# Layer 0 in blocks of 512 tokens, three of them beside the first steps of a recurrence

## The reference, cut to what matters

```python
# x: (2, 1024, 256), N = 64 states
conv = conv_b + sum(x_pad[:, k:k+L, :] * conv_w[k, 0] for k in range(2))
proj = conv @ Wp + bp
B_t, C_t = softplus(proj[..., :N]), tanh(proj[..., N:])
u = x @ Ws + bs
decay = 1.0 + dt * A            # A = -softplus(A_log), dt = softplus(dt_log)
state = decay * state + dt * b_t * u_t      # step by step over 1024 tokens
y = c_t * state
x = x + real(ifft(fft(y @ Wo + bo) @ w)) + bias
```

```python
gate = sigmoid(h @ Wh.T + z_t @ Wz.T + b)
h = tanh(h * leak + gate * z_t)
```

## Time and profile before

| | us |
|---|---|
| median of 3 runs | 3188.67 |
| lowest and highest | 3188.18, 3189.39 |
| the profiled execution, its own time | 3185.09 |
| its span | 3183.8 |
| first `arg` (step 0) in it | 111.73 |
| first `arg` of step 60 in it | 199.50 |

### The profile page before, as it was taken

The page is one execution under the profiler, slowest core; times in us unless marked ns, Lnnn a source line. Parts: engine busy times, 40 slices in busy tenths (PEclk is TensorE's granted clock), DMA queues, the critical chain, the costliest instruction groups (busy, mean ns, idle before and its releaser), DMA issues.

```text
span 3183.8 us, 141437 instructions
## 1 busy us (share of the span) xinstructions
PE 2736.1 (86%) x55104; PEld 2214.4 (70%) x55104; DVE 2172.5 (68%) x13088; ACT 1572.4 (49%) x8437; POOL 338.1 (11%) x457
## 2 busy tenths in 40 slices
PE   4548989989899899998998989988649999979984
PEld 2337878888788888888888888887636666644331
DVE  2558888877777777777777666665437666666238
ACT  2244555556666666666665555543215555531115
POOL 0000010010100101101001010010113444420000
PEclk8555555555555555555555555555559999989997
DMA  2114223322222222322223000000357767332000
GB/s 80 44 53 129 71 84 92 87 64 68 89 89 82 91 63 91 99 80 89 69 88 108 7 17 7 14 17 3 119 189 226 229 193 213 92 129 106 0 0 27
DMA packets 170043, 270.36 MB, mean 85 GB/s; under 512 B 23289, under 2 KB 125580, under 8 KB 167076
## 3 DMA queue, kind: packets, MB, share of 16 engines
q1 hardware_dynamic: 126564, 202.49, 20.3%
q0 software_dynamic: 15312, 33.67, 3.0%
q10 hardware_dynamic: 27504, 25.14, 2.9%
HBM read 170.76 MB, written 98.70 MB: 85 GB/s over the span
## 4 chain that ended last, share of the span: by engine, by line
PE 75%; DVE 12%; ACT 7%; issue 4%; DMA 1%; SPq 1%; POOL 0%; POOLq 0%; ACTq 0%; DVEq 0%
PE bank_h L613 10%; PE bank_r L613 9%; PE bank_g L613 6%; PE bank_z L613 6%; PE bank_h L621 6%; PE work L602 5%; PE bank_r L621 5%; ACT hh_pairs L1085 3%; DVE h_hi L1590 3%; PE work L811 3%; PE bank_z L621 3%; PE bank_z L811 3%; PE bank_h L836 2%; PE work L836 2%; PE work L922 2%
## 5 line engine op out<-in xcount | busy, mean ns | idle before, releaser
L613 PEld LDWEIGHTS bank_r<-h_hi,hi_r 128*128 128x128 f16 x4092 | 206.1, 109 | 331.2 <-DVE h_hi L1590 322.0
L613 PE MATMUL bank_r<-h_hi,hi_r 128*128 128x2 f16 x4092 | 277.0, 171 | 176.2 <-DVE h_hi L1590 169.5
L1590 DVE TENSOR_TENSOR_SCAN h_hi<-zg_pairs,hh_pairs 128x8 f16<-128x8 f32 x1024 | 179.0, 175 | 315.0 <-ACT hh_pairs L1085 267.9
L1085 ACT ACTIVATE hh_pairs<-bank_h 128x4 f32<-128x4 f32 x1024 | 178.6, 174 | 335.4 <-PE bank_h L621 316.5
L1096 ACT ACTIVATE h_hi<-arg 128x4 f16<-128x4 f32 x1024 | 210.1, 205 | 252.9 <-DVE arg L1602 251.2
L613 PE MATMUL bank_g<-h_hi,hi_g 128*128 128x2 f16 x4092 | 254.3, 166 | 68.7 <-ACT h_hi L1096 63.6
L613 PE MATMUL bank_h<-rh_hi,hi_h 128*128 128x2 f16 x4092 | 271.0, 170 | 20.2 <-DVE rh_hi L1575 1.0
L1073 ACT ACTIVATE r_gate<-bank_r 128x4 f32<-128x4 f32 x1023 | 177.2, 173 | 200.8 <-PE bank_r L621 115.0
L621 PE MATMUL bank_h<-rh_lo,hi_h 128*128 128x2 f16 x4092 | 272.7, 170 | 1.4 <-issue 1.4
L621 PE MATMUL bank_r<-h_lo,hi_r 128*128 128x2 f16 x4092 | 267.6, 169 | 1.7 <-DVE h_lo L1606 0.2
L621 PE MATMUL bank_g<-h_lo,hi_g 128*128 128x2 f16 x4092 | 252.7, 166 | 0.0
(11 more groups left out here) (455 smaller groups left out, 7679.0 us busy)
## 6 DMA issues: line engine op xcount, KB each, us to landing
stage<-in_gate_up SPq DMA_DIRECT2D x128, 384.0 KB
stage<-in_down SPq DMA_DIRECT2D x128, 192.0 KB
gu_split<-parts SPq DMA_DIRECT2D x64, 384.0 KB
gu_ring<-gu_split SPq DMA_DIRECT2D x64, 384.0 KB
xt<-x_rows ACTq DMA_DIRECT2D x191, 128.5 KB, 2.3
x_rows<-zero_rows SPq DMA_DIRECT2D x64, 257.0 KB, 3.1
yk<-y_rows SPq DMA_DIRECT2D x16, 1024.0 KB, 4.8
dn_split<-parts SPq DMA_DIRECT2D x64, 192.0 KB
```

The lines of the kernel that those rows point to most:

```text
L613: pe.matmul(o[:, m, step, :], w[:, k, m * P:(m + 1) * P], hi(k), start=False, stop=False, skip_group_check=True)
L1085: act.activation(two(t.hh_pairs[:, :, 0]), gate_in(t.h, c2, s2), ACT.Tanh, scale=scale_of["h"]).then_inc(s.hh_act, 1)
L1590: dve.tensor_tensor_scan(pairs(t.h2_hi), pairs(t.zg_pairs), pairs(t.hh_pairs), 0.0, ALU.mult, ALU.add).then_inc(s.h2hi, 1)
```

## The change

- The loads are split in two groups: five matrices first (`loads0`), then x (`loads_x`, 7 transfers, five of them issued from ACT's queue: `condT`, `feature_cols`, `wp`, `ws`, `bias0`). `ident` goes to the end of `loads1`.
- `conv` of a block is made by ACT (the scaling) and DVE (the shifted addition) together. B and C of a block come out of one product with 128 outputs, `bc`. Abs and Exp go block by block, Ln once for all 2048 columns, Tanh once for block 0 and once for the rest. The bias is added in Abs and in DVE's relu; dt is multiplied in at y.
- Only block 0 goes through drive, scan, y and output ahead of the steps. The maxima and scales of the recurrent weights and the split of `rec_g` are placed around it, and `wom` is finished there. The drives of block 1 follow the output products of block 0 on PE; one bank instead of four is opened ahead of the steps, the other three in steps 56 to 58.
- The other three blocks are pieces in the steps: `LAYER0_A` names DVE's piece of a step (in `place_a`), `LAYER0_PE` PE's (in `beside`).
- To make room, the sums of the feed-forward weights go to steps 25 to 36, the quantising to steps 43 to 55, both DVE halves of a piece in one step, `video_bias` to 30 to 32, the lo-splits to 12 to 17 in `place_b`.
- `stage`, `parts` and some smaller tiles take the memory of layer 0's later blocks. The loads of the feed-forward weights wait for `wom`'s product instead of the last x; the expert pieces wait for the last x too.

```diff
+LAYER0_A = dict(zip((1, 2, 3, 4, 5, 6, 7, 8, 9, 10, 11, 12, 13, 14, 15, 16, 17, 18, 19, 22, 24),
+                    (("sp", 1), ("drive", 1), ("scan", 1, 0), ("scan", 1, 1), ("y", 1), ("sp", 2), ("drive", 2),
+                     ("scan", 2, 0), ("scan", 2, 1), ("y", 2), ("x0", 1, 0), ("sp", 3), ("x0", 1, 1), ("drive", 3),
+                     ("x0", 2, 0), ("scan", 3, 0), ("x0", 2, 1), ("scan", 3, 1), ("y", 3), ("x0", 3, 0), ("x0", 3, 1))))
+LAYER0_PE = dict(zip((1, 2, 3, 4, 5, 6, 7, 8), ((("u", j, q)) for j in (2, 3) for q in range(4))))
+LAYER0_PE.update(zip((9, 10, 11, 12, 13, 14, 15, 16, 20, 21, 22, 23),
+                     (("x0", j, m, q) for j in BLOCKS[1:] for m in range(KH) for q in range(2))))
+OPEN_BANKS = {56: "z", 57: "r", 58: "h"}
+VIDEO_BIAS = (30, 31, 32)
+W_SUMS, W_MEAN, W_SCALE = 25, 37, 42
-    sp.wait_ge(s.d0, X0 + NBLK * KH)
+    sp.wait_ge(s.p0, P0["wom"])
...
+    pe.wait_ge(s.d0, D0["v"])
+    middle(work[2], ((t.w_re, t.v1), (t.w_im, t.v2)))
+    for j in BLOCKS:
+        pe.wait_ge(s.d0, D0["conv", j])
+        if j == 0:
+            pe.wait_ge(s.loads_x, 7 * 16)
+        for k in range(KH):
+            ins = pe.matmul(t.bc_banks[j], t.wp[:, k, :], t.conv[:, k, blk_cols(j)], start=(k == 0), stop=(k == KH - 1))
+        ins.then_inc(s.p0, 1)
+    drives(pe, t, 0, slice(0, BLK)).then_inc(s.p0, 1)
+    middle(work[3], ((t.w_im, t.v1), (t.w_re, t.v2n))).then_inc(s.p0, 1)
...
+    for m in range(KH):
+        pe.matmul(work[2 + m], t.wom[:, m * P:(m + 1) * P], t.cy[:, 0:BLK], start=True, stop=True).then_inc(s.p0, 1)
+    drives(pe, t, 1, slice(0, BLK)).then_inc(s.p0, 1)
...
+    pe.wait_ge(s.setup, READY)
+    open_bank(t.g1)
+    pe.wait_ge(s.d0, D0["x0", 0, KH - 1])
...
+    for j in BLOCKS:
+        soft = t.soft[:, blk_cols(j)]
+        act.wait_ge(s.p0, P0["bc", j])
+        act.activation(soft, t.bc_banks[j][0:NS], ACT.Abs, bias=t.bias0[0:NS, 0:1]).then_inc(s.a0, 1)
+        act.wait_ge(s.a0, A0["abs", j])
+        act.activation(soft, soft, ACT.Exp, scale=-1.0).then_inc(s.a0, 1)
+    act.activation(t.rates_tmp, t.rates_tmp, ACT.Ln, bias=1.0).then_inc(s.a0, 1)
+    act.wait_ge(s.a0, A0["exp", NBLK - 1])
+    act.activation(t.soft, t.soft, ACT.Ln, bias=1.0).then_inc(s.a0, 1)
+    act.wait_ge(s.d0, D0["relu", NBLK - 1])
+
+    act.activation(t.unused, t.ones[0:1, 0:1], ACT.Sigmoid)
+    act.activation(t.cy[0:NS, 0:BLK], t.bc[NS:P, 0:BLK], ACT.Tanh).then_inc(s.a0, 1)
+    act.activation(t.cy[0:NS, BLK:N], t.bc[NS:P, BLK:N], ACT.Tanh).then_inc(s.a0, 1)
...
+    def layer0(what, j, *at):
+
+        cols = blk_cols(j)
+        if what == "sp":
+            dve.wait_ge(s.a0, A0["soft"])
+            v.on(dve.tensor_tensor(t.soft[:, cols], t.soft[:, cols], t.bc[0:NS, cols], ALU.add))
+        elif what == "drive":
+            dve.wait_ge(s.p0, P0["u", j])
+            dve.wait_ge(v.sem, v.n)
+            v.on(dve.scalar_tensor_tensor(t.soft[:, cols], t.u_banks[j][0:NS], t.bias0[0:NS, 2:3], t.soft[:, cols],
+                                          ALU.add, ALU.mult))
...
     def set_up_a(tau):
-        if tau < 6:
-            split_small(GATES[1 + tau // KH], tau % KH)
-        elif tau < 9:
-            gate_bias(tau - 6)
+        if tau in LAYER0_A:
+            layer0(*LAYER0_A[tau])
```

More of the change, by code:

```diff
@@ L322, in place_tiles @@
         t.pad_row = sb("pad_row", [1, NE], I32)
-        t.stage = [sb(f"stage{i}", [P, KH * 2 * INTER]) for i in range(NSTAGE)]
-        t.parts = [sb(f"parts{i}", [P, 2, KH * 2 * INTER], FP16) for i in range(NSPLIT)]
         t.piece_max = sb("piece_max", [P, 2, NE, 3])
@@ L543, in tensor_program, with middle @@
     ins.then_inc(s.p0, 1)
-    pe.wait_ge(s.d0, V_SB)
-    for bank, terms in ((work[2], ((t.w_re, t.v1), (t.w_im, t.v2))), (work[3], ((t.w_im, t.v1), (t.w_re, t.v2n)))):
+    def middle(bank, terms):
         for m in range(KH):
@@ L583, in tensor_program, with drives, open_bank @@
     tensor_layer3(pe, t, s)
+def drives(pe, t, j, cols):
+    x = t.xf[:, :, blk_cols(j)]
+    for k in range(KH):
+        ins = pe.matmul(t.u_banks[j][0:NS, cols], t.ws[:, k, :], x[:, k, cols], start=(k == 0), stop=(k == KH - 1))
+    return ins
 def tensor_recurrences(pe, t, s):
     work = t.work
-    pe.wait_ge(s.setup, READY)
-    for bank in (t.g1, t.z, t.r, t.h):
+    def open_bank(bank):
         for j in range(BLK // P):
@@ L594, in tensor_recurrences @@
                       skip_group_check=True)
+    def layer0(what, j, *at):
+        if what == "u":
+            q, = at
+            ins = drives(pe, t, j, slice(q * P, (q + 1) * P))
+            if q == 3:
+                ins.then_inc(s.p0, 1)
+        else:
+            m, q = at
+            if (m, q) == (0, 0):
+                pe.wait_ge(s.d0, D0["y", j])
+            if q == 0 and j > 1:
+                pe.wait_ge(s.d0, D0["x0", j - 1, m])
+            ins = pe.matmul(work[m][:, q * SLICE:(q + 1) * SLICE], t.wom[:, m * P:(m + 1) * P],
+                            t.cy[:, blk_cols(j)][:, q * SLICE:(q + 1) * SLICE], start=True, stop=True)
+            if q == 1:
+                ins.then_inc(s.p0, 1)
     def input_products(g, c, n):
@@ L973, in scalar_program @@
-    act.activation(t.proj["c"], t.proj["c"], ACT.Tanh).then_inc(s.a0, 1)
+    for dst, src in ((t.condT, halves(A["condT"])), (t.feature_cols, A["feature_cols"]), (t.wp, halves(A["Wp"])),
+                     (t.ws, halves(A["Ws"])), (t.bias0, A["state_cols"])):
+        act.dma_start(dst, src).then_inc(s.loads_x, 16)
+    act.wait_ge(s.loads_x, 7 * 16)
+    for j in BLOCKS:
+        for k in range(KH):
+            ins = act.activation(t.conv[:, k, blk_cols(j)], t.xf[:, k, blk_cols(j)], ACT.Identity,
+                                 bias=t.conv_b[:, k:k + 1], scale=t.condT[:, k, 1:2])
+        ins.then_inc(s.a0, 1)
@@ L990, in scalar_recurrences @@
         act.reg_load(r, (t.down[0:1, i:i + 1] if i < 4 else t.down_neg[0:1]).bitcast(I32))
+    act.wait_ge(s.d0, D0["x0", 0, KH - 1])
+    for k in range(KH):
+        residual(0, k)
     def quantised_weights(n):
@@ L1289, in vector_recurrences @@
     dve.wait_ge(s.setup, READY)
+    for m in range(KH):
+        layer0("x0", 0, m)
     def fill(g, c):
@@ L1619, in vector_table @@
 def vector_table(dve, v, t, s):
+    for q in range(2 * NPIECE, 2 * NPIECE + NSPLIT):
+        dve.wait_ge(store_sem(s, q), 16 * stores_before(q))
     dve.wait_ge(s.count_mm, 1)
```

235 lines of the change are left out of this document (119 added, 116 removed).

## The result

| | before | after |
|---|---|---|
| median, us | 3188.43 (4 runs, 3185.31 to 3189.39) | 3129.77 (4 runs, 3129.18 to 3131.07) |
| profiled execution, us | 3185.09 | 3129.18 |
| first `arg` of step 0 | 111.73 | 49.31 |
| first `arg` of step 60 | 199.50 | 144.78 |
| from there to the end of the span | 2984.3 | 2983.0 |

The ratio is 0.9818 with a 95% interval of 0.9801 to 0.9835. The forecast was 3132.3 in a range of 3122 to 3144. The account of the two spans: 62.4 gained up to the first step, 7.7 paid in steps 0 to 59 (95.5 instead of 87.8), 1.3 gained behind step 60, together 56.0.

What follows compares the result with a forecast made beforehand. PE carries 75% of the chain, nearly all in 1024 recurrence steps left alone; the layer 0 relay ahead is shortened. 3185.09 - 62.4 + 6.0 = 3128.7, median 3.6 above: 3132.3, range 3122 to 3144.

Steps and rivals of the forecast that it cites:

- Loads: Start of layer 0: x lands at 12.5 us, between 11.0 and 14.16, with the first and half the middle products hidden under it.
- Six issues sooner: Load of x on SP: issued sixth and seventh instead of twelfth and thirteenth, 3.1 us earlier.
- The rest of the path: Layer 0 from convolution to the first arg, forecast at 49.3 instead of 111.73; with the loads, 62.4 us gained.
- The steps: Blocks 1 to 3 beside the early steps: DVE time over its 0.60 us slots is paid, 6.0 us in all.
- PE waits in them for DVE's y or x: Sign of being wrong: in steps 1 to 24, PE is held up by DVE's y or x.
- the 20 pieces cost nothing: PE's pieces in the steps, 0.86 us each, fit in about 1.1 us free; without that cover up to 17.
- The median: Median of the runs taken as 3.6 us above the profiled execution, raising 3128.7 to 3132.3.
- The clock stays low: Rival in layer 0: bc products never reach full clock, 13.8 us instead of 8.9; +4.9, 3137; 10%.
- Better: Rival: drives and output products at full clock (-3.5), x at 11.0, steps hide more; 3126; 10%.
- No room on DVE: Rival in the steps: DVE's 21 operations paid whole, 13.4 us instead of 5.8; +7.6, 3140; 10%.
- The step is not freed: Rival: the first step waits for all of layer 0, some 25 us of serial remainder less 6.0; 3151; 2%.
- The slower one, moved tiles: Rival: new tile addresses beside DMAs lengthen the 1024 steps; 0.055 us each cancels the gain, 0.08 gives 3214; 2%.

Runs made afterwards that it cites:

- base: The changed kernel with two registers, used in the expert stage alone, loaded with bounds; 3129.59 us, ratio 0.9824 to the kernel before.
- dve_narrow: base with DVE's 21 pieces of blocks 1 to 3 on 8 columns instead of 512; one execution 3129.94 us, steps 0 to 59 in 90.30.
- pe_narrow: base with PE's pieces of blocks 2 and 3 on 2 columns instead of 128 or 256; one execution 3131.04 us, steps 0 to 59 in 94.66.
- serial: base with all DVE and PE pieces of blocks 1 to 3 run before step 0, none beside the steps; 3143.52 us, 13.9 over base.
- best_filled: base with layer 2 set-up pieces moved off layer 0's steps, maxima between relus, drives of blocks 1 to 3 in PE's pauses; 3204.85 us, ratio 0.9789 to before.
- k128: The kernel before the change with y and wom padded by zero rows from 65 to 128 operand rows; one execution 3182.74 us, beside 3189.79 unpadded.
- drives_early: base with the drives of block 1 moved into PE's pause ahead of the folded matrix product; one execution 3129.11 us, first arg at 46.91.

## Why the prediction was right, step by step

The first `arg` came at 49.31 where 49.3 was forecast, but the terms did not all hold; two misses cancel.

| term | predicted | profile after |
|---|---|---|
| x lands | 12.5 | 14.0 |
| first product of `bc` | 15.4 | 17.2 |
| four blocks of `bc` | 8.9 | 8.4 |
| abs and relu | 1.6 | 1.6 |
| maxima to scales | 3.9 | 3.8 |
| a1, a2n, rates | 1.1 | 0.9 |
| block 0 on DVE | 3.8 | 3.7 |
| splits and `wom` | 2.6 | 2.4 |
| output products, drives, bank | 7.5 | 7.9 |
| input products to `arg` | 4.5 | 3.3 |

- **Loads** failed. "Six issues sooner" did not bring x forward: `w_im`, issued at 2.76, took 6.25, and x behind it landed at 14.0 (12.8 to 14.8 in other executions with this order of loads). The issue time was not what bounded it. That the first products and half of the middle ones lie under the load failed with it: PE could begin at 9.0 only, when the five matrices were there, and its queue (3.69 + 0.8 + 3.67) ended at 17.2, level with the convolution. The stage starts 1.8 late.
- **The rest of the path** held within 0.5 for each term, except the last. The exact sum therefore owes something to luck: 1.8 too late at the start and 1.2 too early at the end. The input products and the first step's products were taken at half clock from the earlier trace rows but the clock came back within the former (1.52 instead of 1.83), and the latter ran at full clock (1.07 instead of about 1.9): 1.2 less. In base it came back even sooner; 47.5 to 49.5 is what this stage does.
- **The steps**: 7.7 instead of 6.0. DVE's sum held (steps 1 to 10: 15.84, predicted 12.9 + 2.8), and dve_narrow shows that it is DVE's. Four things were missed. Step 20 waits for y (1.90 instead of 1.3). The prediction had named "PE waits in them for DVE's y or x" as a sign that it would be wrong; in this one step it did, and the other steps with a product of y show no such wait. In steps 12, 14 and 16 the lo-split waits on DVE's own semaphore for the operation just ahead, which it does not need, and these steps are 1.80 to 1.86 instead of 1.74. Steps 21 and 23, with a PE piece and nothing of layer 0 on DVE, are 1.36 where 1.27 was implied (pe_narrow: 1.28 and 1.27). So "the 20 pieces cost nothing" was not quite so: a piece takes 1.04 on PE and not 0.86, and 1.1 us were not free there. And step 42, where a reciprocal stands ahead of a quantising half, is 0.24 longer.
- **Behind step 60** the prediction expected no change. The 1.3 gained lie within what other executions of the same code show (2982 to 2988); the tick after step 60 alone varies from 3.6 to 4.8, by DVE's wait for the first expert piece.
- **The median** was put 3.6 above the profiled execution, as in the runs of before. In the changed kernel it is 0.6 above. That offset was chance and not a property of the kernel. It made the forecast 3.0 too high; the sum without it, 3128.7, was 0.5 under the profiled execution's 3129.18, where the 1.7 missed in the steps and the 1.3 behind step 60 nearly cancel. Together these are the 2.5 by which the forecast was too high.
- **Rivals.** "The clock stays low" did not come: in every execution the first block's product took 3.2 to 3.8, and the clock rose during it or the second block's. "Better" did not come either: x landed at 14.0, and the output products and drives of the changed kernel ran at half clock (3.78 and 3.68). "No room on DVE" did not come (7.7, not 13.4). "The step is not freed" was mispriced: serial shows the remainder at 17 to 19, not 25. The slower one, moved tiles, did not show: 342 steps in the 700 us from 300 on, 343 before, and the time behind step 60 did not grow.

The Trainium skill ("TensorE: Matmul & The Clock Gate", section "Why this matters for your kernels") advises matmuls without pauses to gain and hold the full clock. The prediction weighed this against the earlier trace rows and found that it fails in its plain form. best_filled agrees with the advice: from 26 to 42 us PE's longest pause is 0.62, and the clock stayed at 1.00, through 1.98 us of 65-row products too. k128 bears on why it fell short in the earlier trace rows: what was busy there had 65 operand rows.

The other page that was weighed ("VectorE: DVE Perf Modes", section on the TRN2 errata) would, by the prediction's estimate, have made the sum 2 us lower. The 0.74 us of 64x512 at 34.83 and 0.61 at 31.83 speak for the trace's durations. That section asks for tiles of 512 elements or more, which these blocks are, so it does not speak against them as the prediction had it.

## What to carry to other kernels

A stage ahead of a loop is worth rebuilding before it is worth overlapping: here 43 to 45 of 57 us came from the order and the fusing inside it, and 12 to 14 from work put beside the steps. A slot beside a step has one price per engine: fill it with one piece up to its size and never with two while other steps are empty, and look for the next engine's limit directly under the first. If PE waits for another engine in a pause of a few microseconds, move real products into the pause; in best_filled they ran at the full clock and kept it for what came behind. Fill the whole pause: with part of it filled (drives_early) the clock fell all the same.
